# An attention kernel on one core: the place of the residual add in GpSimd's order

## What is computed

```python
q = (jnp.einsum('bfe,oe->bfo', x, Wq) + bq).reshape(B, F, H, D)
k = (jnp.einsum('bfe,oe->bfo', x, Wk) + bk).reshape(B, F, H, D)
v = (jnp.einsum('bfe,oe->bfo', x, Wv) + bv).reshape(B, F, H, D)
att = jnp.einsum('bfhd,bghd->bhfg', q, k) * scale
att = jax.nn.softmax(att, axis=-1)
out = jnp.einsum('bhfg,bghd->bfhd', att, v).reshape(B, F, H * D)
res = jnp.einsum('bfe,oe->bfo', x, Wr) + br
return jax.nn.relu(out + res)
```

## Time and profile before

| | |
|---|---|
| median of three executions | 921.47 us (921.42 to 921.93) |
| the profiled execution's own time | 923.84 us |
| its span, first to last instruction | 921.1 us |
| TensorE matmul busy | 892.3 us, 97% |
| GpSimd busy | 872.1 us, 95% |
| ScalarE, VectorE busy | 770.6 us (84%), 726.7 us (79%) |
| mean granted clock of TensorE | 0.996 |

### The profile page before, as it was taken

One profiled execution on the slowest core, in us unless ns is written; L12 is line 12 of the kernel. 1 busy time (PEld: TensorE's weight loads), 2 busy tenths in 40 slices (PEclk: granted clock), 3 DMA queues, 4 the chain that ended last, 5 costly groups with the idle time before them and its releaser, 6 DMA issues.

```text
span 921.1 us, 67888 instructions
## 1 busy us (share of the span) xinstructions
PE 892.3 (97%) x30208; PEld 626.7 (68%) x30208; DVE 726.7 (79%) x2066; ACT 770.6 (84%) x1541; POOL 872.1 (95%) x1028
## 2 busy tenths in 40 slices
PE   6999999999999999999999999999999999999996
PEld 4667666767666776676666667666667766767664
DVE  5878777878787877888887878787878887878785
ACT  4888888888888888888888888888888888888886
POOL 3999999999999999999999999999999999999997
PEclk9999999999999999999999999999999999999998
DMA  4333333333333333333333333333333333333321
GB/s 120 97 110 117 113 105 110 115 107 112 118 112 107 116 111 111 111 117 109 115 112 105 110 111 111 112 112 112 117 111 112 112 120 108 115 110 112 111 83 67
DMA packets 67429, 101.20 MB, mean 110 GB/s; under 512 B 13632, under 2 KB 46656, under 8 KB 67136
## 3 DMA queue, kind: packets, MB, share of 16 engines
q1 hardware_dynamic: 66704, 96.72, 34.7%
q10 hardware_dynamic: 432, 0.15, 0.1%
HBM read 54.88 MB, written 41.94 MB: 105 GB/s over the span
## 4 chain that ended last, share of the span: by engine, by line
PE 93%; POOL 3%; issue 2%; DVE 1%; DMA 0%; ACT 0%; POOLq 0%; ACTq 0%
PE vr_bank L422 24%; PE o_bank L475 22%; PE s_buf L406 19%; PE o_bank L386 15%; PE s_buf L452 7%; PE vr_bank L433 6%; POOL y_sum L191 1%; POOL m_diag L183 1%; POOL q_bd L199 1%; PE o_bank L390 0%; DMA biases<-bias_in 0%; ACT y_rows L238 0%; POOLq L39 0%; DVE s_buf L325 0%; PE vr_bank L438 0%
## 5 line engine op out<-in xcount | busy, mean ns | idle before, releaser
L183 POOL TENSOR_TENSOR m_diag<-m_split,ident 128x640 bf16<-128x640 bf16 x256 | 323.1, 1262 | 32.2 <-DVE m_split L336 30.1
L191 POOL TENSOR_TENSOR y_sum<-rv,y_att 128x512 f32<-128x512 f32 x256 | 303.9, 1187 | 1.9 <-DVE y_att L347 1.9
L199 POOL TENSOR_SCALAR q_bd<-q_flat,consts 128x320 f32<-128x320 f32 x512 | 267.6, 537 | 11.2 <-DVE kT L320 11.1
L422 PE MATMUL vr_bank<-w_cols,xT 64*128 64x128 f32 (+1 forms) x3072 | 269.0, 308 | 0.1
L258 ACT ACTIVATE rv<-vr_bank 128x1024 f32<-128x1024 f32 x256 | 260.4, 1017 | 0.1
L325 DVE TRANSPOSE_TENSOR_REDUCE s_buf<-s_buf 128x20 f32<-128x640 f32 x256 | 221.6, 866 | 47.8 <-PE s_buf L406 47.7
L475 PE MATMUL o_bank<-rv,pT 64*40 64x33 f32 x16384 | 229.6, 202 | 12.1 <-issue 8.4
L406 PEld LDWEIGHTS s_buf<-q_bd,kT 64*40 64x40 f32 x8192 | 151.5, 113 | 116.2 <-issue 115.1
L475 PEld LDWEIGHTS o_bank<-rv,pT 64*40 64x40 f32 x16384 | 192.9, 117 | 54.4 <-issue 17.9
L320 DVE TENSOR_SCALAR kT<-o_bank,biases 128x320 f32<-128x320 f32 x256 | 140.9, 550 | 89.1 <-PE o_bank L390 89.0
L406 PE MATMUL s_buf<-q_bd,kT 64*40 64x80 f32 x8192 | 200.5, 233 | 1.4 <-issue 1.1
(11 more groups left out here) (31 smaller groups left out, 466.0 us busy)
## 6 DMA issues: line engine op xcount, KB each, us to landing
xT<-xT_in SPq DMA_DIRECT2D x512, 104.0 KB, 2.7
y<-y_rows SPq DMA_DIRECT2D x512, 80.0 KB
w_cols<-w_in SPq DMA_DIRECT2D x1, 192.0 KB, 2.6
vr_bias<-vr_bias_in ACTq DMA_DIRECT2D x1, 128.0 KB, 3.3
consts<-consts_in ACTq DMA_DIRECT2D x1, 20.0 KB, 2.4
biases<-bias_in ACTq DMA_DIRECT2D x1, 1.0 KB, 3.8
```

Source lines behind the costliest of these rows:

```text
L183: pool.tensor_tensor(m_diag[:], m_split[:, place % 2].unsqueeze(2).to_broadcast([P, BLOCKS, QUAD]), ident[:].unsqueeze(1).to_broadcast([P, ...
L191: pool.tensor_tensor(y_sum[:, n % 3].rearrange("r (a d) -> r a d", d=DIM), rv[:, place % 4, RESIDUAL * HEADS:(RESIDUAL + SLOTS) * HEADS, 0 ...
L199: pool.tensor_scalar(q_bd[:, place % 4, :, s], q_flat[:, place % 2].rearrange("d (b f) -> d b f", f=FIELDS), consts[:, C_HEAD + s:C_HEAD + ...
L422: return nc.tensor.matmul(blocks(half, first, step)[:, 0:count], xT[rows, place % 8, PAIR * pair:PAIR * pair + P], w_cols[rows, 1:1 + coun ...
```

## The change

GpSimd's turn is put into another order. The residual add of step n-4 comes between the diagonals of step n-2 and the masked copies of the queries of step n; it stood behind the copies. No instruction is added or taken away, and every wait stays with its instruction. The four turns behind the loop (diagonals, then residual add) are as before.

```diff
             def group(n, place):
                 if not before(n, 2):
                     diagonals(n - 2, place + 6)
-                query_columns(n, place)
                 if not before(n, 4):
                     add_residual(n - 4, place + 4)
+                query_columns(n, place)
```

## The result

The changed kernel takes 975.76 us (median of four executions, 975.07 to 976.40) against 921.44 us (920.92 to 921.93) for the kernel before: the ratio is 1.0595, with a 95% interval of 1.0568 to 1.0623. That is 54.3 us slower. The forecast was 989.5 us, with a range of 958 to 1009. A ratio is always taken from executions in the chip's faster state alone, while a median is of all executions; with the 20 waits and in the control with the moved wait one of four was in the slower state, with the eight waits two.

The account below looks back on a forecast made before the run. TensorE was taken as the bound, GpSimd close behind. A two-turn loop of 3.14 + 3.40 + 0.90 = 7.44 us plus 0.138 gave 3.79 us per turn against 3.518, +68 us over 251 turns: 989.5 us, range 958 to 1009.

Parts of the forecast that it names:

- The bound before: TensorE bounds the kernel before, at 97% busy, with GpSimd close behind at 95%; an undisturbed turn is 3.38 us.
- the slack: Between the copies' end and the next kT: 0.45 us, against a move of 1.13, so L390 is 0.68 us late.
- the loop: From kT over GpSimd's diagonals, add and copies to kT two turns on: 7.44 us, or 3.72 per turn.
- 3.14, 3.40, 0.06 and 0.90 us: kT to next diagonals 3.14; diagonals, add and copies 3.40; copies' end to L390's weight load 0.06, to kT 0.90.
- The disturbances: Extra 0.138 us per turn in scores and attend, added once per two-turn loop: 7.58, or 3.79 us per turn.
- the first rival: Disturbances vanish, as TensorE's sequencer might have its next code while waiting at line 389: 3.72 us per turn, 972 us; chance 0.16.
- the case to which I gave 0.60: The forecast's own case: two-turn loop with disturbances on top, 3.79 us per turn, median 989.5 us.
- The doubled disturbances: Waiting at line 389, TensorE's sequencer can't run ahead into the scores: twice 0.138, 7.72 per pair, 1007 us; chance 0.13.
- The clock: Gaps of some 0.3 us a turn cost TensorE its full clock: 5.5 us a turn, near 1420 us; chance 0.02.
- The delay taken once: L390 is 0.68 us late in turn 5 and not again: 922 us, not slower; chance 0.05.
- every turn pays: The loop is one turn long, so 0.68 us is lost each turn: +171, 1092 us; chance 0.04.
- The new wait row: Sign in the profile after: L390 on TensorE waits for POOL q_bd, about 68 us in all.

Follow-up runs that it names:

- the 20 waits: Kernel before with 20 always-met waits at the end of each TensorE turn, no work added: 1006.02 us, ratio 1.0884.
- the control with the moved wait: Kernel before, old GpSimd order, with TensorE's wait for the copies moved from ahead of L390 to ahead of the scores: 967.87 us, ratio 1.0408.
- the eight waits: Kernel before with eight always-met waits per TensorE turn ahead of the bias matmul L433: 967.68 us, ratio 1.0420.
- the memset run: Changed kernel with one more GpSimd instruction, a memset of a scratch tile, between the add and the copies: 1015.03 us, ratio 1.0946.
- The exchanged waits: TensorE's wait for the copies put ahead of the scores, the exponentials' wait ahead of L390: changed order 948.44 us, kernel before 948.23 us.
- the memset behind the add: Kernel before with an extra GpSimd memset behind the add, lengthening GpSimd's turn but not the loop: 964.67 us, ratio 1.0403.
- the wait right ahead of the scores: Changed kernel with TensorE's wait for the copies moved from ahead of L390 to ahead of the scores: 976.35 us, ratio 1.0504.
- the merged shift: Kernel before with the shift's four matmuls made two on the whole array, same result: 929.52 us, ratio 1.0044.

## Why the prediction was right, and what it mis-sized

- **The bound before, the slack, the loop: right.** Each of 3.14, 3.40, 0.06 and 0.90 us has its row in the trace after. The pair is 7.45 against 7.44 forecast, the turns alternate 3.39 and 4.06 at the start as forecast and are nearly alike later on, and the memset run shows that one extra us on GpSimd costs half a us per turn. The exchanged waits show that the cost hangs on where TensorE waits for the copies: there the new order takes 948.44 us and the old one 948.23.
- **The disturbances: the term that was mis-sized.** The step read "The disturbances come on top" and added 0.138 us to each pair, 7.58. Measured, the mean pair is 7.458: 0.018 on top. Without that term the working gives 972 us, the first rival's number, against 975.76; the forecast had 989.5. So the case to which I gave 0.60 came out 14 us too long, and the rival with 0.16 came nearest, inside the same range. The sign that I had named for it is there too: L475 fell to 211.7/256 = 0.83 us a turn and didn't keep its 0.90. The forecast called this rival's mechanism code that is there by then. The runs support the code: the gaps keep to one place in 256 instructions, and each ends 1.2 to 1.7 us behind a packet of the instruction queue. They give pace rather than the stop at line 389 as the cure, since gaps also go where TensorE stops elsewhere (23 with the memset behind the add).
- **What spoke against that rival was no argument.** "The stalls fall into scores and attend, behind the wait" is true and says nothing: one packet of code comes for each 256 instructions, which is about one a turn, and a longer turn leaves it more time wherever the stop stands.
- **The doubled disturbances** didn't come in the changed kernel. With the wait right ahead of the scores there were 128 gaps in place of 93, but its control with early copies had 126.
- **The clock** stayed at its full tenth in the changed kernel (mean 0.996). **The delay taken once** and **every turn pays** are refuted by pairs of 7.45.
- **Three signs were misread in advance.** TensorE's busy share rose to 98% where I said some 90%, since L386 and L390 no longer overlap. The new wait row holds 17.8 us and not 68. GpSimd's idle time ahead of the diagonals is 84 us against 98, which is 251 x (3.729 - 3.40) = 83 with the turn as it came.
- The add that is done earlier brought nothing, as forecast (it starts 27.43 - 26.42 = 1.01 us earlier, not 1.03). No kernel tried was faster than the kernel before; the merged shift came nearest, at 1.0044.

## What to carry to other kernels

Before an instruction is moved on an engine with slack in its sum, look for the first waiter behind what is moved, and follow the chain until it returns to its start; divide the loop's length by the number of turns it spans, and compare that with the turn. Look at whether a wait stands ahead of what reads the data or earlier: here it stood one pair of matmuls too early, and the new order cost 54 us with it and 0.2 us without. But moving it is no free gain: both moves tried here cost time of their own in the old order (42 and 27 us against the kernel before in the same sets of runs), one by an added instruction and one by a wait that wasn't yet met. Small stalls of an engine near its bound may vanish when another bound takes over: don't add them to a new loop unseen.

## What the runs showed of the hardware that was not expected

TensorE's late code sets in at the pace of this kernel: with 236 instructions in 3.38 us there are 93 gaps, 0.26 us at the lower tenth and 0.56 at the upper, and at 3.88 us only the 2 of the drain. TensorE resumes 1.2 to 1.7 us behind the end of a packet of code. The Trainium skill (Runtime: NRT & Kernel Launch, section Instruction fetch mechanics) says that crossing a block is mostly hidden; these traces differ for TensorE at its densest. A wait that is always met isn't free there either: one more per turn cost 1.0% ahead of the bias matmuls and 4.1% ahead of the scores, there with stops of up to 2.5 us, after some of which the granted clock was 0.5 for 3.4 us.
